# ALiBi attention: the distance bias of two heads at once by 64x64 quarter tiles, with smaller identity multiples

## The chip, the cores and the metric

The kernel runs on one core of one Trainium2 chip. The metric is device time in microseconds, from one launch of the program; less is better. TensorE (PE), VectorE (DVE), ScalarE (ACT) and GpSimd (POOL) run side by side and are ordered by semaphores; SyncE (SP) only issues transfers. PEld is TensorE's weight load, PE its matmul.

## The reference

Six layers follow each other on x (16 sequences, 256 tokens, 128 features): a local-attention feed-forward block, an ALiBi attention, the same feed-forward block again, a mixture of experts, a linear attention, the experts again. Only the ALiBi attention matters here. Per sequence it has 16 heads of width 8:

```python
scores = jnp.einsum('bhid,bhjd->bhij', q, k) / scale
scores = scores + _alibi_bias(N_HEADS, seq_len, M_SLOPE, x.dtype)[None]   # -|i - j| * 0.5**h
attn = jax.nn.softmax(scores, axis=-1)
out = jnp.einsum('bhij,bhjd->bhid', attn, v)
```

## The kernel before

The program is written out by hand for each engine, with semaphores between them: `ffn(0)`, `attn()`, `ffn(1)`, `moe(0)`, `lin()`, `moe(1)`. There is no planner; each engine issues its instructions in the order of its own Python loop.

The set-up comes first. `shape_constants` computes tables on the host; the part up to `slope_eye` is loaded into the tile `stage` by one transfer of ScalarE's queue (L812), followed on the same queue by small loads (`lo_q`, `lo_k`, `block`, q and k scales). VectorE waits for all of them (L848) and converts the parts to bf16: masks (L851), `relub` (L852), `sel` (L853), `slopeb` (L854), and goes on with the tables and weights until the first `ffn` starts at about 60 us.

In `attn()` all three engines run a loop over k (a sequence, in -2 to 19) and p (8 steps, two heads each). In a step TensorE computes two things (`scores`, L1559). The *plain* scores of sequence k, heads 2p and 2p+1, go to PSUM banks 0 and 1: q is the stationary operand, so rows are queries; VectorE takes their row maximum (`s_max`, L1068), which frees the banks for step p+1. The *turned* scores, of heads that lie 11 steps back (u = 8k + p - 11), go to banks 4 and 5 with keys on the rows; ScalarE takes their exponential (`exps`, L692), which frees them. Every score product has a contraction of 32 rows (8 of q high, q low, position and maximum rows), and the row group of a head is given by its number, so that plain and turned products of four heads lie in four different groups of 32 rows of the array.

The linear part of the bias, -m|i-j| for the off-diagonal blocks, comes in with the position rows of these products. In the two diagonal blocks of 128x128 that form is wrong by 2m max(i-j, 0) or its mirror. This is mended by the distance products: the stationary operand is `slopeb[:, h, :]`, a 128x128 multiple -2m of the identity for head h, the moving one a 128x128 table `relub` of max(p-f, 0) or max(f-p, 0). There are four of them for the plain scores (two heads, two diagonal blocks, L1584) and four for the turned (L1591). The last of the four raises the semaphore on which `s_max` or `exps` waits.

After `scores`, the step's other work follows on TensorE (L1645 to L1665): `attend` (L1603) at odd p; `m_T` (L1616) and `proj` (L1641) at p = 0, `v_proj` (L1555) at 1, `mean` (L1531) and a half of `qk` (L1544 to L1547) at 2, the other half and `var` (L1535) at 4, `o_rows` (L1627) at 6, `o_cols` (L1636) at 7. VectorE adds to its maximum `m_add` (L1080) and `x_out` (L1092) at p = 0, `v_out` (L1061) at 1, `center` (L1047) at 2, `low` (L1056) at 3 and 5, `normed` (L1051) at 5, `o_norm` (L1086, L1087) at 6, `m_split` (L1074, L1075) at 7. ScalarE copies q and k (`high`, L687) at 3 and 5, before the exponentials of the step; the other copies (L697, L702) and `square`, `rstd` (L678, L682, L683) stand between them.

Of the kernel before, what the change touches and what calls it, by code (L numbers as in the profile page):

```python
# [20 lines left out]
BF16 = mybir.dt.bfloat16  # L21
# [4 lines left out]
SEQS, T, D = 16, 256, 128  # L26
LANES = 2
TILES = T // 128
P = 128
# [12 lines left out]
AH, ADH = 16, 8  # L42
# [22 lines left out]

def shape_constants():

    t = np.arange(T, dtype=np.float32)
    half = np.arange(0, DH, 2, dtype=np.float32)
# [12 lines left out]
    p, f = np.arange(P)[:, None], np.arange(P)[None, :]  # L82
# [30 lines left out]
    slope_eye = np.concatenate([-2.0 * m * eye for m in slopes], 1)  # L113
# [4 lines left out]
    parts = dict(rot=rot, masks=np.concatenate([st0, st1, s0, s1], 1), relu=np.concatenate([relu_pf, relu_fp], 1),  # L118
# [9 lines left out]
def build(nc, io, at):  # L128
    ctx = ExitStack()
    with ctx:  # L130
        def sb(name, shape, dt=F32, on=ctx):
            return on.enter_context(nc.sbuf_tensor(name, shape, dt))
# [40 lines left out]
        relub = sb("relu_bf", [P, 2, P], BF16)  # L173
        slopeb = sb("slope_eye_bf", [P, AH, P], BF16)
# [659 lines left out]
        def _(dve):  # L834
            steps = [0]

            def link(ins):

                steps[0] += 1
                ins.then_inc(chain, 1)  # L840
                dve.wait_ge(chain, steps[0])
# [10 lines left out]
            link(dve.tensor_copy(relub[:, :, :].rearrange("p a b -> p (a b)"), part("relu")))  # L852
# [438 lines left out]
        def _(pe):  # L1291
# [235 lines left out]
            def attn():  # L1527
# [30 lines left out]

                def scores(k, p, u):  # L1559
# [20 lines left out]
                    if plain:  # L1580
                        for b in range(2):
                            for t in range(TILES):
                                a = t * T + t * P
                                last = pe.matmul(PS[:, b, a:a + P], slopeb[:, 2 * p + b, :], relub[:, 1 - t, :],  # L1584
                                                 start=False, stop=True, skip_group_check=True)
                        last.then_inc(a_s, 1)
                    if turned:
                        for b in range(2):
                            for t in range(TILES):
                                a = t * T + t * P  # L1590
                                last = pe.matmul(PS[:, 4 + b, a:a + P], slopeb[:, 2 * r + b, :], relub[:, t, :],  # L1591
                                                 start=False, stop=True, skip_group_check=True)
                        last.then_inc(a_st, 1)
# [280 lines left out]
```

## Time and profile before

| | |
|---|---|
| Median of 3 runs | 2494.72 us (2492.01 to 2496.49) |
| Profiled execution | 2494.18 us, its span 2492.4 us |
| PE busy | 2238.0 us (90%), 21606 products |
| PEld busy | 1670.2 us (67%) |
| DVE busy | 1709.9 us (69%) |
| ACT busy | 1465.2 us (59%) |
| POOL busy | 1095.6 us (44%) |
| Distance products, plain (L1584) | 53.0 us, 512 records, mean 229 ns |
| Distance products, turned (L1591) | 50.1 us, 512 records, mean 221 ns |
| TensorE's granted clock | 0.952 of full on average |

A product's record covers its own passage through the array, so the records of neighbouring products overlap and their sum is more than the time that they take. In the order of time, neighbouring instructions of one line are merged into one row with their number (x4); its start is that of the first and its length runs to the end of the last. Of a row the bracket at the end says how long the engine was idle before it, and what released it. A share of 1.00 in the clock's column is 2.4 GHz, 0.50 is 1.2 GHz. The attention stage lies between about 905 and 1280 us.

### The profile page before, as it was taken

The numbers are of one execution on the slowest core, as the hardware profiler recorded it, in microseconds if no ns is written. First come the engines' busy times: TensorE is split into PE (matmuls) and PEld (weight loads), VectorE is DVE, ScalarE is ACT, GpSimd is POOL, SyncE is SP. The second block draws the span as 40 slices with busy tenths as digits, with TensorE's granted clock in tenths as the row PEclk, the third lists the DMA queues.
The fourth block names the chain that finished last, engine by engine and source line by source line (L and its number), as shares of the span: only waits on it lengthen the run. The fifth ranks groups of instructions, "written<-read, shape, count | busy, mean of one in ns | idle before, by whom it ended". The sixth has DMA issues, their size and how long they took to land. (4 is left out here: it accounts for less than half of the span.)

```text
span 2492.4 us, 52712 instructions
## 1 busy us (share of the span) xinstructions
PE 2238.0 (90%) x21606; PEld 1670.2 (67%) x21606; DVE 1709.9 (69%) x2815; ACT 1465.2 (59%) x2389; POOL 1095.6 (44%) x800
## 2 busy tenths in 40 slices
PE   1799999999999969999969999999999997597968
PEld 1577777777777646666646777777777775495758
DVE  3677777778888636777737777777788784563556
ACT  0476767666676515555546677766676664363635
POOL 4655555656555210000025565656555560550245
PEclk8799999999999969999989999999999998698979
DMA  7000000069999970000000000000000002221022
GB/s 152 1 1 1 2 1 1 1 76 119 131 147 147 147 85 1 2 2 2 2 1 1 2 1 1 1 2 2 1 2 1 1 1 68 55 70 38 33 74 81
DMA packets 211362, 90.88 MB, mean 36 GB/s; under 512 B 79700, under 2 KB 206721, under 8 KB 210996
## 3 DMA queue, kind: packets, MB, share of 16 engines
q1 hardware_dynamic: 202596, 72.27, 21.8%
q0 software_dynamic: 6080, 11.76, 1.5%
q10 hardware_dynamic: 2448, 3.48, 0.7%
q8 instruction: 173, 2.83, 0.5%
q14 instruction: 65, 0.53, 0.1%
HBM read 24.51 MB, written 63.41 MB: 35 GB/s over the span
## 5 line engine op out<-in xcount | busy, mean ns | idle before, releaser
L477 POOL TENSOR_TENSOR work<-work,rot_tables 128x512 f32<-128x512 f32 x256 | 446.5, 1764 | 440.7 <-ACT work L581 440.7
L485 POOL TENSOR_TENSOR work<-work 128x1024 f32<-128x1024 f32 x128 | 305.2, 2384 | 13.0 <-DVE work L911 3.1
L911 DVE TENSOR_TENSOR work<-work,rot_tables 128x1024 f32<-128x1024 f32 x128 | 162.2, 1268 | 112.2 <-ACT work L581 112.2
L1068 DVE TENSOR_REDUCE small<-psum 128x4 f32<-128x1024 f32 x128 | 156.5, 1223 | 95.5 <-PE psum L1584 95.4
L1310 PE MATMUL psum<-qkv_w_hi,h_hi 128*128 128x512 f32 x384 | 182.7, 476 | 18.9 <-POOL h_lo L504 16.4
L1464 PE MATMUL psum<-centered,ffn_w 128*128 128x256 f32 x768 | 190.3, 399 | 6.1 <-DVE centered L972 2.9
L928 DVE TENSOR_TENSOR work<-work,small 128x1024 f32<-128x1024 f32 x128 | 159.5, 1248 | 51.2 <-ACT small L595 47.0
L692 ACT ACTIVATE work<-psum 128x1024 f32<-128x1024 f32 x128 | 131.2, 1025 | 102.2 <-PE psum L1591 102.2
L1402 PE MATMUL psum<-work 64*128 64x128 f32 (+1 forms) x2048 | 180.8, 307 | 0.0
L492 POOL TENSOR_TENSOR y_all<-centered,squared 64x256 f32<-64x256 f32 x64 | 48.7, 761 | 295.0 <-ACT squared L641 292.4
L1464 PEld LDWEIGHTS psum<-centered,ffn_w 128*128 128x128 f32 x768 | 145.8, 196 | 36.2 <-DVE centered L972 17.7
L1435 PE MATMUL psum<-work,v 128*32 128x192 f32 (+1 forms) x4096 | 162.9, 299 | 0.0
L609 ACT ACTIVATE work<-psum 128x768 f32<-128x768 f32 (+1 forms) x192 | 154.6, 872 | 3.6 <-PE psum L1402 3.5
L917 DVE TENSOR_REDUCE small<-qk_squares 128x16 f32<-128x1024 f32 x128 | 154.7, 1208 | 0.4 <-ACT qk_squares L586 0.4
L1312 PE MATMUL psum<-qkv_w_hi,h_lo 128*128 128x512 f32 x384 | 153.2, 399 | 0.0
L1311 PE MATMUL psum<-qkv_w_lo,h_hi 128*128 128x512 f32 x384 | 153.1, 399 | 0.0
L601 ACT ACTIVATE work<-psum 128x1024 f32<-128x1024 f32 x64 | 65.7, 1026 | 144.8 <-PE psum L1329 144.8
L546 POOL DMA_INDIRECT h_area<-rows,position x64 | 62.2, 972 | 199.7 <-DVE position L1150 173.4
L1402 PEld LDWEIGHTS psum<-work 64*128 64x128 f32 x2048 | 144.1, 189 | 0.0
L581 ACT ACTIVATE work<-psum 128x1024 f32<-128x1024 f32 x128 | 130.3, 1018 | 22.3 <-PE psum L1312 21.5
L750 ACT ACTIVATE qk_squares<-psum,work 128x128 f32<-128x128 f32 x312 | 89.0, 368 | 89.7 <-PE psum L1725 89.7
L528 POOL CAST h_hi<-centered 128x256 fp32r<-128x256 f32 x16 | 6.3, 396 | 302.9 <-DVE centered L1051 302.9
(285 smaller groups left out, 5718.6 us busy)
## 6 DMA issues: line engine op xcount, KB each, us to landing
h_area<-mean_weights SPq DMA_DIRECT2D x24, 2048.0 KB
tile_x<-h_area SPq DMA_DIRECT2D x39, 128.5 KB, 2.1
stage<-in_consts ACTq DMA_DIRECT2D x1, 3009.0 KB, 12.6
tile_x<-h_area SPq DMA_DIRECT2D x39, 64.5 KB, 1.8
work<-in_x SPq DMA_DIRECT2D x4, 512.0 KB, 27.4
expert_w<-in_ew SPq DMA_DIRECT2D x1, 2048.0 KB, 8.6
expert_w<-in_ew SPq DMA_DIRECT2D x8, 256.0 KB, 6.9
work<-y_tokens SPq DMA_DIRECT2D x4, 512.0 KB, 6.1
```

Source lines behind the costliest of these rows:

```text
L477: last = pool.tensor_tensor(b[:, :, :, o_], a[:, :, :, i_], tab[:, l, 1, t, :, o_].unsqueeze(2).to_broadcast([P, 2, HEADS, 32]), ALU.mult)
L485: pool.tensor_tensor(rC[:, t, :], rC[:, t, :], rB[:, t, :], ALU.add).then_inc(f_sum, 1)
L609: act.activation(PT[:, hs, a:a + w].rearrange("p (h b) j -> p b h j", b=2), PS[:, bs, 0:m * w].rearrange("p b (h j) -> p b h j", h=m), ACT ...
L911: dve.tensor_tensor(g(rC[:, t, :]), g(rA[:, t, :]), tab[:, l, 0, t, :, :].unsqueeze(2).to_broadcast([P, 2, HEADS, DH]), ALU.mult)\
L917: dve.tensor_reduce(sm[0][:, 16 * t:16 * t + 16], sq[:, t, :].rearrange("p (g d) -> p g d", d=DH), AX, ALU.add).then_inc(f_ss, 1)
L928: dve.tensor_tensor(c_, c_, sm[0][:, 96 + 16 * t:112 + 16 * t].unsqueeze(2).to_broadcast([P, 16, DH]), ALU.mult).then_inc(f_nrm, 1)
L1068: dve.tensor_reduce(dst, PS[:, 0:2, :].rearrange("p b (t j) -> p b t j", t=TILES), AX, ALU.max, negate=True).then_inc(a_smax, 1)
L1310: pe.matmul(out, hi, w_hi, start=True, stop=False)
L1312: return pe.matmul(out, lo, w_hi, start=False, stop=True)
L1402: last = pe.matmul(PS[:, bs[h % 2], o:o + w], kT[rows_(h), h // 2, j * P:(j + 1) * P], qT[rows_(h), h // 2, i0:i0 + w], start=False, stop= ...
L1435: last = pe.matmul(PS[32 * q:32 * q + 32, (4, 2)[a], z * T + lo:z * T + hi], V[i % 2][:, j, d:d + 32], PT[:, 4 * a + q, src:src + hi - lo] ...
L1464: last = pe.matmul(PS[:, b, o:o + T], fw[:, l, o2 + c * P:o2 + (c + 1) * P], ycen[:, :], start=True, stop=True)
```

## The change

Both tables are laid out anew and the distance products are issued on quarters of the array.

`slope_eye` holds 64x64 multiples of the identity instead of 128x128 ones: in rows 0 to 63 those of the even heads, in rows 64 to 127 those of the odd, 8 pairs x 64 columns (512 columns instead of 2048). `relu` holds max(p-f, 0), max(f-p, 0), max(p-f, 0) side by side, its upper 64 rows once for both row halves and then its lower 64 rows for both (768 columns instead of 256).

`distances` issues four products where there were four: for each half of the output rows and each of the two heads one with a contraction of 64 rows, 64 output rows and 256 columns, which are both diagonal blocks of the head (blocks 0 and 3 of the bank's four blocks of 128). The head gives the row half of the array and the bank, the half of the output gives the column half of the array. The order is half 0 of both heads, then half 1 of both. The semaphore is raised by the last, as before.

```diff
--- before.py
+++ after.py
@@ -61,6 +61,11 @@
 EPS = 1e-5
 MASKED = -1e30
 LN_SET = "natural_log_exp_and_others"
+
+
+def halves_of(a):
+
+    return np.concatenate([np.tile(a[0:64], (2, 1)), np.tile(a[64:P], (2, 1))], 1)
 
 
 def shape_constants():
@@ -110,12 +115,12 @@
             k_cols[2, c, r + ROW_MHI] = k_cols[2, c, r + ROW_MLO] = 1.0
         lo_q[r + 8:r + 16] = -1.0
         lo_k[r + 16:r + 24] = -1.0
-    slope_eye = np.concatenate([-2.0 * m * eye for m in slopes], 1)
+    slope_eye = np.concatenate([np.concatenate([-2.0 * m * eye[0:64, 0:64] for m in slopes[r::2]], 1) for r in range(2)], 0)
     block = (p // LDH == f // LDH).astype(np.float32)
     order = np.tile(np.arange(NE, 0, -1), (P, 4))
     before = (p < f).astype(np.float32)
     row_no = np.tile(np.repeat(np.arange(ROWS), NE), (P, 1))
-    parts = dict(rot=rot, masks=np.concatenate([st0, st1, s0, s1], 1), relu=np.concatenate([relu_pf, relu_fp], 1),
+    parts = dict(rot=rot, masks=np.concatenate([st0, st1, s0, s1], 1), relu=halves_of(np.concatenate([relu_pf, relu_fp, relu_pf], 1)),
                  q_cols=q_cols.reshape(P, -1), k_cols=k_cols.reshape(P, -1), q_vals=q_vals, k_vals=k_vals, lo_row=lo_row,
                  sel=sel.reshape(P, -1), slope_eye=slope_eye, eye=eye, lo_q=lo_q, lo_k=lo_k, block=block, order=order, before=before, row_no=row_no)
     at, n = {}, 0
@@ -170,8 +175,8 @@
         ms0, ms1 = masks[:, JW:JW + P], masks[:, JW + P:2 * JW]
         sel = sb("m_rows_bf", [P, HEADS, P], BF16)
         tab = sb("rot_tables", [P, DEPTH, 2, TILES, 2, DH])
-        relub = sb("relu_bf", [P, 2, P], BF16)
-        slopeb = sb("slope_eye_bf", [P, AH, P], BF16)
+        relub = sb("relu_bf", [P, 2, 3, P], BF16)
+        slopeb = sb("slope_eye_bf", [P, AH // 2, 64], BF16)
         lo_q, lo_k = sb("lo_q", [P, 1]), sb("lo_k", [P, 1])
         block = sb("block", [P, P])
         raw_qk = work[1][:, 4 * 4 * P:6 * 4 * P]
@@ -849,7 +854,7 @@
             link(dve.tensor_copy(eyeb[:, :], eye[:, :]))
             link(dve.memset(mneg[:, :, :], 0.0))
             link(dve.tensor_copy(masks[:, :], part("masks")))
-            link(dve.tensor_copy(relub[:, :, :].rearrange("p a b -> p (a b)"), part("relu")))
+            link(dve.tensor_copy(relub[:, :, :, :].rearrange("p a k b -> p (a k b)"), part("relu")))
             link(dve.tensor_copy(sel[:, :, :].rearrange("p h j -> p (h j)"), part("sel")))
             link(dve.tensor_copy(slopeb[:, :, :].rearrange("p h j -> p (h j)"), part("slope_eye")))
 
@@ -1556,6 +1561,15 @@
                                          start=True, stop=True)
                     last.then_inc(a_v, 1)
 
+                def distances(b0, pair, first):
+                    for half in range(2):
+                        for r in range(2):
+                            k_, o_ = slice(64 * r, 64 * r + 64), slice(64 * half, 64 * half + 64)
+                            blocks = PS[o_, b0 + r, :].rearrange("p (a c) -> p a c", c=P)[:, 0::3, :]
+                            last = pe.matmul(blocks, slopeb[k_, pair, :], relub[k_, half, first:first + 2, :],
+                                             start=False, stop=True, skip_group_check=True)
+                    return last
+
                 def scores(k, p, u):
                     plain, turned = 0 <= k < SEQS, 0 <= u < 8 * SEQS
                     m, r = u // 8, u % 8
@@ -1578,19 +1592,9 @@
                                 pe.matmul(PS[:, 4 + b, t * T:(t + 1) * T], ks[m % 3][row(r, b), r // 2, t * P:(t + 1) * P],
                                           qs[m % 3][row(r, b), r // 2, :], start=t == 0, stop=False, skip_group_check=True)
                     if plain:
-                        for b in range(2):
-                            for t in range(TILES):
-                                a = t * T + t * P
-                                last = pe.matmul(PS[:, b, a:a + P], slopeb[:, 2 * p + b, :], relub[:, 1 - t, :],
-                                                 start=False, stop=True, skip_group_check=True)
-                        last.then_inc(a_s, 1)
+                        distances(0, p, 1).then_inc(a_s, 1)
                     if turned:
-                        for b in range(2):
-                            for t in range(TILES):
-                                a = t * T + t * P
-                                last = pe.matmul(PS[:, 4 + b, a:a + P], slopeb[:, 2 * r + b, :], relub[:, t, :],
-                                                 start=False, stop=True, skip_group_check=True)
-                        last.then_inc(a_st, 1)
+                        distances(4, r, 0).then_inc(a_st, 1)
 
                 def attend(w):
                     k, c = w // 4, w % 4
```

## Rows read from the trace of the kernel before

**Rows 1.** Stretches of the attention stage: us, busy us (x instructions) of PE, PEld, DVE, ACT, POOL; PEclk, DMA, GB/s
```profile
966.00:1250.00 284.00, 265.98 (x3354) 191.21 (x3350) 208.81 (x251) 166.75 (x210) 13.43 (x24) 1.00 0.01 2
905.00:966.00 61.00, 48.62 (x414) 37.16 (x414) 35.14 (x40) 16.71 (x21) 3.35 (x6) 0.72 0.13 16
```

**Rows 2.** Order of time, PE: start us, us, engine, line; the proj product, eleven sequences apart
```profile
978.65 0.43 PE L1641 MATMUL psum<-work,attn_w_vo 128*128 128x256 f32 x1
...
1213.66 0.43 PE L1641 MATMUL psum<-work,attn_w_vo 128*128 128x256 f32 x1
```

**Rows 3.** Order of time, PE and PEld: scores and distance products of step p = 2
```profile
1046.29 0.39 PE L1574 MATMUL psum<-k_slots,q_slots 32*128 32x256 f32 x2
...
1046.52 0.28 PE L1578 MATMUL psum<-q_slots,k_slots 32*128 32x256 f32 x2
...
1046.72 0.23 PEld L1584 LDWEIGHTS psum<-relu_bf,slope_eye_bf 128*128 128x128 bf16 x4
1046.73 0.40 PE L1584 MATMUL psum<-relu_bf,slope_eye_bf 128*128 128x128 bf16 x4
...
1046.96 0.39 PE L1591 MATMUL psum<-relu_bf,slope_eye_bf 128*128 128x128 bf16 x4
...
1047.13 0.30 PEld L1531 LDWEIGHTS psum<-x_all,mean_weights 128*128 128x128 f32 x2
```

**Rows 4.** Order of time, PE: changes of tile form and waits in other steps
```profile
1044.33 0.39 PE L1591 MATMUL psum<-relu_bf,slope_eye_bf 128*128 128x128 bf16 x4
1044.64 1.07 PE L1603 MATMUL psum<-work 128*32 128x256 f32 x16
...
1053.07 0.36 PE L1544 MATMUL psum<-h_hi,attn_w_hi 128*128 128x256 f32 x1
...
1062.39 0.44 PE L1636 MATMUL psum<-eye,work 128*128 128x128 f32 x2
```

**Rows 5.** Order of time, DVE, of one sequence
```profile
1042.26 1.23 DVE L1068 TENSOR_REDUCE small<-psum 128x4 f32<-128x1024 f32 x1 [0.52 <-PE psum L1584]
1043.40 1.21 DVE L1080 TENSOR_TENSOR q_slots<-q_slots,psum 128x1024 fp32r<-128x1024 f32 x1
...
1044.93 1.22 DVE L1068 TENSOR_REDUCE small<-psum 128x4 f32<-128x1024 f32 x1
...
1051.69 1.27 DVE L1056 SCALAR_TENSOR_TENSOR q_slots<-q_slots,lo_q,psum 128x1024 fp32r<-128x1024 f32 x1
...
1056.45 1.23 DVE L1068 TENSOR_REDUCE small<-psum 128x4 f32<-128x1024 f32 x1 [2.35 <-PE psum L1584]
...
1059.12 1.22 DVE L1068 TENSOR_REDUCE small<-psum 128x4 f32<-128x1024 f32 x1
...
1061.27 1.23 DVE L1068 TENSOR_REDUCE small<-psum 128x4 f32<-128x1024 f32 x1 [0.21 <-PE psum L1584]
```

**Rows 6.** Order of time, ACT, step p = 3
```profile
1049.78 1.02 ACT L687 ACTIVATE q_slots<-psum 128x1024 fp32r<-128x1024 f32 x1 [1.37 <-PE psum L1547]
1050.78 1.02 ACT L692 ACTIVATE work<-psum 128x1024 f32<-128x1024 f32 x1
```

**Rows 7.** Order of time, PE and ACT, a turned step after the last plain one
```profile
1253.51 0.40 PE L1591 MATMUL psum<-relu_bf,slope_eye_bf 128*128 128x128 bf16 x4
...
1253.94 1.02 ACT L692 ACTIVATE work<-psum 128x1024 f32<-128x1024 f32 x1 [0.92 <-PE psum L1591]
```

**Rows 8.** Set-up: a stretch, then VectorE's first conversions in order of time
```profile
0.00:10.00 10.00, 0.00 (x0) 0.00 (x0) 0.00 (x0) 0.00 (x0) 9.15 (x14) 1.00 0.82 303
...
34.62 0.23 DVE L849 CAST eye_bf<-eye 128x128 bf16<-128x128 f32 x1 [34.62 <-DMA qk_squares<-in_k_scale]
...
35.66 0.29 DVE L852 CAST relu_bf<-stage 128x256 bf16<-128x256 f32 x1
...
36.72 1.23 DVE L854 CAST slope_eye_bf<-stage 128x2048 bf16<-128x2048 f32 x1
```

**Rows 9.** A stretch before the body of the stage (columns as in rows 1)
```profile
955.00:960.00 5.00, 4.24 (x68) 2.53 (x60) 3.72 (x5) 2.52 (x4) 0.00 (x0) 0.91 0.00 0
```

## Prediction

> **What bounds the kernel now.** I read the busy share of TensorE first, then its share and clock by stretches, then the order of instructions inside one sequence of the attention stage. TensorE is the busiest engine of the whole program (90% of the span, in the table above). The change touches only two places: the set-up of the constants (the first 60 us) and the ALiBi stage, which runs from 905 us to 1280 us. In the body of that stage (966 to 1250 us) TensorE is busy 266 of 284 us at full clock, VectorE 209 and ScalarE 167 [rows 1]; in its head the clock is half of the time the low one (0.72 on average). So at first sight TensorE sets the pace, but 94% is an average over eight unlike steps, and what a shorter product is worth depends on what each step waits for.
>
> The body is strictly periodic: eleven sequences between two launches of the same projection take 1213.66 - 978.65 = 235.0 us, 21.37 us each [rows 2]. One sequence has eight steps p. A step issues eight score products in 32-row tiles, four distance products of the plain scores (L1584), four of the turned ones (L1591), and then the step's other work: an attend product at odd p, and m_T and proj, mean and qk, qk and var, o_rows at p = 0, 2, 4, 6.
>
> **The parts of one step.** S is the start of the step's scores, 1046.29 in [rows 3]. There the second set of score products starts at S+0.23 and its 256 columns at 2.4 GHz (clock 1.00) are streamed 0.107 us later, at S+0.34. The first weight load of the distance products comes at 1046.72 = S+0.43: 0.09 to 0.10 us in which nothing streams, because the array passes from 32-row tiles to the full array. The four plain products (4 in 0.40 us, 0.22 of it one product's own record, so 0.06 apart) end at S+0.84, the turned ones at S+1.06. The next load in the same full form follows at once (1047.13 = S+0.84). Where the next work has another tile form it follows later: L1591 ends at 1044.33+0.39 = 1044.72, its last product started 0.22 before that, at 1044.50, streamed 0.05, and L1603 starts at 1044.64, again 0.09 late [rows 4]; the turned group ended there at S+1.06, so L1603 starts at about S+0.99. So a change of form costs 0.10 us, seen in both directions.
>
> **What the change makes of it.** Each group of four 128-column products over the full array becomes four of 256 columns, each on a 64x64 quarter. The trace has no 64x64 product, so I bound it. From below: if all four quarters run together, a group is 256 columns = 0.107 us, against 4 x 0.055 = 0.22 us now; it can't be less. The nearest rows are for running together: four 32-row tiles (two rows of two products, 0.01 us apart, [rows 3]) and four 32-column tiles (16 products of L1603 in 1.07 us [rows 4], where 16 one after the other at the same 256 columns of two-pass f32 would take 3.4 us). Rows are split in the one and columns in the other; both at once is not shown. From above: two at a time 0.215 us, one at a time 0.43 us. I take 0.107 us, since both halves of the claim are shown. The first load in a new form is exposed: for 128 columns of f32 it makes the first score record 0.10 us longer than the second (0.38 against 0.28 [rows 3]). For 64 columns I take 0.05, with 0 and 0.10 as ends.
>
> Then a step becomes: load at S+0.43, plain group streamed by S+0.43+0.05+0.107+0.01 (three starts after each other) = S+0.60, its end 0.17 later (a 128-column record of 0.22 less its 0.053 of streaming), S+0.77 instead of S+0.84: **0.07 us earlier for VectorE's maximum**. The turned group ends 0.11 later, at S+0.88 instead of 1.06: **0.18 earlier for ScalarE's exponentials**. The array is free for another form at S+0.71+0.10 = S+0.81. At odd p, where another form follows anyway, this is 0.18 before the present 0.99. At even p the change adds a change of form that wasn't there: the f32 load now begins at S+0.84 and its product streams 0.107 later, S+0.95; afterwards S+0.81+0.107 = S+0.92, only **0.03 earlier**.
>
> The Trainium skill, TensorEngine Tiling (Array Packing), "Key Properties", says that a change of tiling mode drains the engine; this speaks against the change at the even steps, and the trace agrees with its 0.10 us. The Trainium skill, TensorE: Matmul & The Clock Gate, "Measured speedup vs the span model", has row and column tiles composed, at about 4 ns a tile; no run here shows it, and by it the group would be the 0.107 us plus 0.01. The same page, "Weight-path perf modes", gives the fast load only to 128 columns, and in "LDWEIGHTS" a load of its columns over 1.2 GHz, an estimate of 0.053 us for 64; the sum would be the same by it.
>
> **Which of this lies on the path, step by step.** A step starts when the later of three is there: TensorE free, the maximum of the step before (0.14 us after its end), the exponentials of the step before.
> - p = 0 to p = 2: the maximum of p = 0 (1042.26), m_add L1080 (1043.40), x_out L1092 and the maximum of p = 1 (1044.93 + 1.22 = 1046.15) are one unbroken chain on VectorE [rows 5], and 0.14 later p = 2 starts, at 1046.29. TensorE would have been ready at the same moment; it gains 0.27 here and gets 0.07. Gain 0.07.
> - p = 2 to 3: the qk block on TensorE, an even step. 0.03.
> - p = 3 to 4: ScalarE copies q high (1049.78 + 1.02) and only then does the exponentials (1050.78) [rows 6]; the earlier product is hidden by the copy. 0.
> - p = 4 to 5: the qk block (L1544 at 1053.07 [rows 4]) waits for `low` (1051.69 + 1.27 [rows 5]), which stands behind the maximum of p = 3. 0.07.
> - p = 5 to 7: from the maximum of p = 5 (1056.45) over `low` and `normed` to the maximum of p = 6 (1059.12) VectorE is unbroken [rows 5]. 0.07.
> - p = 7 to 0: TensorE: attend, then o_cols (1062.39 [rows 4]), then scores; odd step, 0.18. VectorE's maximum (1061.27 + 1.23 + 0.14 = 1062.64) is 0.11 behind at present and 0.07 earlier too, so it doesn't stop it.
> Sum 0.42 us of 21.37. The stretch in which plain and turned run together, 942 to 1249 us, has 14 such periods: **5.9 us**. TensorE alone saves 4 x 0.18 + 4 x 0.03 = 0.84 a period; half of it is lost to VectorE and ScalarE.
>
> Head: 11 steps of plain scores alone; in some 8 the maximum sets the pace, 0.07 each, 0.5 us (at the low clock everything doubles and the gain is no smaller). Tail: 11 turned steps, L1591 at 1253.51 and exponentials at 1253.94 [rows 7]. The four products now take 0.43 to that point; then it is 0.05 + 0.107 + 0.01 + 0.17 + 0.03 = 0.37. 11 x 0.06 = **0.7 us**.
>
> Set-up: VectorE converts the constants in an unbroken chain from 34.62 us on. slope_eye shrinks from 2048 to 512 columns, relu grows from 256 to 768. The two conversions (0.29 for 256 and 1.23 for 2048 columns, hence 0.52 us per 1000) fall from 1.52 to 0.42 + 0.56 us: **0.5 us** [rows 8]. The stage load loses 1024 columns, 0.52 MB; at the 303 GB/s of the first 10 us that is 1.7 us of transfer. The chain starts on the last of the small loads behind it, which may follow by all of it or by nothing; I take 0.8.
>
> Sum 5.9 + 0.5 + 0.7 + 0.5 + 0.8 = 8.4 us. The profiled execution took 2494.18 us (span 2492.4 and 1.8 around it), so 2485.8; the median of the runs is 0.5 higher, which gives **2486.3 us**. Ends of its own: load exposed for 0 and the whole transfer gained, 0.04 us more on four links of a period and each loop, 8.4 + 2.2 + 1 + 0.9 = 12.5, 2482; load 0.10 (0.05 more on each: -3.5) and nothing from the transfer, 4.1 us, 2490.6. Own range 2482 to 2491.
>
> **Rivals.**
> - *Two quarters at a time.* A group takes 0.215. The plain group ends at S+0.88 (0.04 later than now), exponentials start 0.02 later, odd steps are 0.03 and even ones 0.17 later. By the same links: 0.04 + 0.17 + 0.02 + 0.04 + 0.04 + 0.03 = 0.34 a period, 14 x 0.34 + 1 less 1.3 for the set-up = 4.5 us slower, 2499. Against it stand the two rows of four tiles together; for it only that the mix is not shown. The point of balance lies at about 0.165 us a group.
> - *One at a time*: 0.43 a group. Then TensorE bounds every step: loops through the exponentials grow by 0.45, even steps by 0.60. Some 3.3 us a period, 14 x 3.3 + 6 - 1 = 51 us slower, 2546. This is the case clearly on the other side; it decides as soon as quarters that share rows or columns exclude each other, which no row suggests.
> - *The clock falls inside the body.* TensorE would be busy some 88% instead of 94%. The clock was 0.91 in a stretch of 5 us with 4.24 us busy [rows 9], and it stayed full through the whole body, with 94%. If it fell in one qk block of each sequence, 16 products of 256 columns would take 0.107 us more each, 1.7 us: 14 x 1.7 = 24, less 8 gives 16 us slower, 2510. Against it: the columns that each quarter streams grow, only the time shrinks.
> - *VectorE absorbs more than I give it*: only the set-up and the ends remain, and 0.1 to 0.2 a period: 4 us faster, 2491.
> - That the quarters aren't used as such (the products fall back to the full array) comes out as one at a time.
>
> **Chances.** Forecast 0.60, VectorE absorbs 0.12, two at a time 0.15, the clock 0.07, one at a time 0.03, better than 2481 0.03. What a measurement of this kernel can tell from no change is about 0.2%, 5 us: 2489.7 and 2499.7 are the borders. Faster: nine tenths of the forecast, a third of the absorbed case, the 0.03: 0.62. Slower: the clock, one at a time and a third of two at a time, 0.15. Same 0.23. For 8 in 10 the range takes in two at a time: 2481 to 2500.
>
> **What would show it.** In the changed profile: the four quarter records of a group starting within 0.02 us of each other and the second group 0.11 after the first (right) or 0.2 and more (rival); the first load of the group 0.10 after the scores; the maximum at S+0.80, the exponentials at S+0.92; a period of 20.95 us; p = 3 to 4 unchanged; clock 1.00 from 966 to the end of the body; the conversion of slope_eye in 0.4 us and the chain starting near 33.8. A period over 21.3 or a low clock in the body would prove me wrong.

## The result, and the profile after

The changed kernel took 2486.93 us (median), the kernel before 2495.12 us in the same comparison: 8.2 us less by the medians; the ratio is 0.9971 [0.9961, 0.9981], which is 7.2 us. One of the ten executions of each kernel ran far longer than its others (7251.18 and 2851.13 us): they are in these medians, but not in the ratio. The profiled execution took 2481.03 us, with a span of 2478.9 us. The forecast was 2486.3 us. The sum hit the total; several of its terms were off, in both directions, and those are what the experiments were for. The kernels before and after have two profiles each, the other forms one, and a form whose time isn't given below was executed once and is read by its trace alone.

The stretch 966 to 1250 us of [rows 1] can't be laid beside the same stretch of the changed kernel, because the stage starts 4 us earlier and is shorter, so that this stretch now holds most of its tail. What does compare is the proj product (order of time, TensorE), against [rows 2]:

```profile
969.39 0.43 PE L1645 MATMUL psum<-work,attn_w_vo 128*128 128x256 f32 x1
...
1197.64 0.43 PE L1645 MATMUL psum<-work,attn_w_vo 128*128 128x256 f32 x1
```

Eleven sequences take 1197.64 - 969.39 = 228.25 us: **a period of 20.75 us**. Before the change it was 21.37, and 20.95 had been forecast. The step p = 2, all engines in order of time, against [rows 3] and the second row of VectorE's chain in [rows 5]:

```profile
1013.11 1.22 DVE L1073 TENSOR_REDUCE small<-psum 128x4 f32<-128x1024 f32 x1
...
1014.38 0.39 PE L1588 MATMUL psum<-k_slots,q_slots 32*128 32x256 f32 x2 [0.16 <-DVE small L1073]
...
1014.61 0.28 PE L1592 MATMUL psum<-q_slots,k_slots 32*128 32x256 f32 x2
1014.82 0.14 PEld L1569 LDWEIGHTS psum<-relu_bf,slope_eye_bf 64*64 64x64 bf16 x8
1014.82 0.41 PE L1569 MATMUL psum<-relu_bf,slope_eye_bf 64*64 64x256 bf16 x8
1015.16 0.30 PEld L1536 LDWEIGHTS psum<-x_all,mean_weights 128*128 128x128 f32 x2 [0.20 <-issue]
...
1015.17 1.23 DVE L1073 TENSOR_REDUCE small<-psum 128x4 f32<-128x1024 f32 x1 [0.49 <-PE psum L1569]
1015.28 1.03 ACT L697 ACTIVATE work<-psum 128x1024 f32<-128x1024 f32 x1 [1.63 <-PE psum L1569]
```

With S = 1014.38, the maximum starts at S+0.79 (before: 1042.26 - 1041.39 = 0.87), the exponentials at S+0.90 (before: 1047.39 - 1046.29 = 1.10, ScalarE), the next full-array load at S+0.78 (before S+0.84). The eight products of both groups span 0.41 us, where the two groups of four took from 1046.73 to 1047.35.

The tail (turned steps alone) and the set-up answer [rows 7, 8], in order of time:

```profile
1237.28 0.30 PE L1569 MATMUL psum<-relu_bf,slope_eye_bf 64*64 64x256 bf16 x4
...
1237.64 1.02 ACT L697 ACTIVATE work<-psum 128x1024 f32<-128x1024 f32 x1 [0.84 <-PE psum L1569]
```

```profile
31.80 0.23 DVE L854 CAST eye_bf<-eye 128x128 bf16<-128x128 f32 x1 [31.80 <-DMA qk_squares<-in_k_scale]
...
32.85 0.56 DVE L857 CAST relu_bf<-stage 128x768 bf16<-128x768 f32 x1
...
34.17 0.43 DVE L859 CAST slope_eye_bf<-stage 128x512 bf16<-128x512 f32 x1
```

The two conversions now take 0.99 us instead of 1.52, as forecast. In the tail it is 0.36 us from products to exponentials instead of 0.43, with 0.37 forecast, and a step takes 1.86 us (1236.85 to 1238.71) instead of 1.94 (1253.08 to 1255.02). This is at full clock; later in the same tail a step takes 2.95 us (1245.61 to 1248.56) in a stretch at the low clock.

**The stage in three parts** (head, body, tail). I cut it at the first turned score product, the last plain one, and the first product of the next stage. Before, then after (us, busy us (x instructions) of PE, PEld, DVE, ACT, POOL; PEclk, DMA, GB/s):

```profile
905.30:941.30 36.00, 27.64 (x158) 22.19 (x158) 19.28 (x22) 3.13 (x5) 2.24 (x4) 0.59 0.21 25
941.30:1249.00 307.70, 285.96 (x3588) 205.50 (x3590) 223.70 (x266) 180.20 (x224) 14.55 (x26) 0.99 0.01 2
1249.00:1280.00 31.00, 23.67 (x253) 13.96 (x249) 6.24 (x12) 16.88 (x20) 0.00 (x0) 0.94 0.01 1
```

```profile
901.30:935.00 33.70, 25.39 (x162) 18.98 (x162) 19.28 (x22) 3.13 (x5) 2.24 (x4) 0.65 0.22 28
935.00:1233.10 298.10, 266.23 (x3591) 169.53 (x3590) 222.71 (x266) 178.78 (x224) 14.54 (x26) 0.99 0.01 2
1233.10:1265.10 32.00, 24.99 (x252) 13.04 (x249) 6.33 (x12) 16.88 (x20) 0.00 (x0) 0.84 0.01 1
```

Two profiles of before (head, body, tail 36.0, 307.7, 31.0 and 35.8, 306.0, 29.8) have means 35.9, 306.9, 30.4. Four of the quarter form (33.7, 298.1, 32.0; 33.9, 297.5, 35.1; 34.0, 297.5, 35.1; 34.0, 298.3, 32.0: this one, again, pad and eight, below) have 33.9, 297.9, 33.6. So **the body gives 9.0 us, the head 2.0, the tail takes 3.2 back**, and with 0.5 from the conversions that is 8.3 us. TensorE's clock in the tail is 0.84 and 0.72 in the changed forms, 0.94 and 1.00 before. In the first profile of the changed kernel the low clock lies here:

```profile
1224.00:1230.80 6.80, 5.58 (x64) 2.25 (x56) 3.22 (x3) 3.32 (x4) 0.00 (x0) 0.50 0.01 2
1241.10:1251.30 10.20, 9.07 (x70) 4.79 (x68) 0.00 (x0) 4.69 (x5) 0.00 (x0) 0.50 0.00 0
```

The first of the two is still in the body, and the steps in it take 2.23, 2.59 and 3.16 us instead of 2.07 each, 1.8 us in all. The three other profiles of the quarter form have low clock in the same place.

### The profile page after: what moved, and what is told of

The parts are those of the page before. It is cut to its first block and busy times, and to the rows that moved or that the text cites. A ratio compares the mean times of both kernels' runs of the same rounds, so it can differ in the third digit from the quotient of the medians.

```text
span 2478.9 us, 52712 instructions
## 1 busy us (share of the span) xinstructions
PE 2222.0 (90%) x21606; PEld 1634.3 (66%) x21606; DVE 1710.0 (69%) x2815; ACT 1464.7 (59%) x2389; POOL 1094.9 (44%) x800
## 3 DMA queue, kind: packets, MB, share of 16 engines
q10 hardware_dynamic: 2448, 2.95, 0.6%
## 5 line engine op out<-in xcount | busy, mean ns | idle before, releaser
L697 ACT ACTIVATE work<-psum 128x1024 f32<-128x1024 f32 x128 | 131.0, 1024 | 90.6 <-PE psum L1569 90.3
L591 ACT ACTIVATE qk_squares<-work 128x1024 f32<-128x1024 f32 x128 | 135.4, 1058 | 2.0
```

## Experiments

The period below is always the one between two proj products eleven sequences apart.

**again**: the changed kernel once more.

> The changed kernel once more, to set the body of the attention stage against the rest. The body must show the 20.75 us period again. Theory A (14 periods of 0.62 us and the shorter conversions, 9.2 us, arrive at the end): ratio 0.9963. Theory B (some of it is given back where the clock is low for part of the time, in the ends of this stage and in the expert stages after 2080 us, because their low stretches fall differently from run to run): ratio 0.9975 to 0.999, and the trace has more low-clock time after 2080 us than the 105 us of before. First conversion somewhere in 31.8 to 34.6 us, with no relation to the size of the transfer.

2494.32 us against 2501.72 us, ratio 0.9968 [0.9955, 0.9982], period 20.75 (967.08 to 1195.32). The gain is there again. The interval holds the ratios of both theories (0.9963, 0.9975), so it doesn't decide between them. From the end of the stage to the end of the program the profiles of the changed kernel take 1213.8 and 1222.4 us (again), those of the kernel before 1212.4 and 1219.1 (before2): what lies behind the stage varies by as much as the gain.

**before2**: the kernel before once more, for its stage.

> The kernel before once more, word for word, for a second profile of it. Theory A (start of the conversions and length of the expert stages vary from run to run, whatever the kernel): first conversion between 31.7 and 33.2 us as in all other runs rather than at 34.6, and from 2080 us on a time or low clock unlike the first profile's, period 21.37 all the same. Theory B (both belong to the kernel before): 34.6 us again, and the shortest expert stages.

Period 21.36 (975.13 to 1210.08), time 2496.34; the first conversion of the set-up starts at 32.81 us, where it was 34.62 in the first profile of the same program. So the start of VectorE's chain moves by 1.8 us, and the part behind the stage (above) by 6.7 us, from one execution to another of the same kernel.

**pad**: 1024 unused columns in the stage load, so that it is as large as before.

```diff
-    parts = dict(rot=rot, masks=..., relu=halves_of(...),
+    parts = dict(rot=rot, masks=..., relu=halves_of(...), pad=np.zeros((P, 1024)),
```

> The changed kernel with 1024 columns of zeros added to the set-up transfer, so that it is as long as before; nothing else differs. Theory A (the shorter transfer lets VectorE's first conversion start at 31.8 us instead of 34.6): the start goes back to 34.3 to 34.9 and the first product of the feed-forward block comes at 59.6 instead of 56.8 us (before 60.2); the whole run loses 2.8 us of the gain, about 5.5 us faster than before, ratio 0.9978. Theory B (the start varies from run to run whatever the length): it stays near 31.8, the ratio near 0.9967.

The first conversion starts at 32.88 us; in the changed kernel it was 31.80 and 31.71 (again), in others with the small load 32.98 (plain_only) and 32.18 (eight). That is neither theory's number. Beside the 1.8 us by which before itself moves, one pair of profiles can't tell what the 0.52 MB costs. Over all fourteen profiles of this page, the five with the load of before (before, before2, before_halfmax, pad, and rows_only with its wider table) start between 32.25 and 34.62 us, 33.14 on average, and the nine with the small load between 31.71 and 33.00, 32.24 on average. The 0.9 us between the averages is near the 0.8 that I took, but the two ranges overlap, so the effect is likely and not shown. The time was 2489.98 against 2492.61, ratio 0.9992 [0.9978, 1.0007], and that I can't explain: its period is 20.75, its stage 366.6 us, within 0.1 of that of again, and its profiled execution (2489.76 us) took what again's did (2489.89). What differs between the two comparisons, on the same chip, is the kernel before, 2492.61 in one and 2501.72 in the other. It stays open whether the padding costs something outside the stage or whether the kernel before was at its best there. The part behind the stage doesn't single pad out: 1218.7 us, between the two profiles of the changed kernel.

**plain_only** and **turned_only**: only one of the two groups uses quarters; the other uses the old full-array products, with tables built in the set-up.

```diff
-                        distances(4, r, 0).then_inc(a_st, 1)
+                        distances_full(4, r, True).then_inc(a_st, 1)    # plain_only
...
-                        distances(0, p, 1).then_inc(a_s, 1)
+                        distances_full(0, p, False).then_inc(a_s, 1)    # turned_only
```

> Only the plain distance products by quarters, the turned ones as before, over the full array (their tables are built by 18 more small VectorE instructions in the set-up, some 4 us, so only the period of the stage is compared). Theory A (a change of tile form costs 0.10 us, and now stands between the two groups too): the maximum starts at S+0.80 as in the changed kernel, but the exponentials at S+1.13, later than before (1.10); the period is 21.34 us, hardly better than the 21.37 before. Theory B (each group brings its half of the gain, 0.31 us): 21.06.

> Only the turned distance products by quarters, the plain ones as before (same longer set-up). Theory A (form change between the groups): maximum at S+0.87 as before, exponentials at S+1.12, period 21.4 us, no better than the 21.37 before. Theory B (each group brings half): 21.06.

Periods 21.23 (977.86 to 1211.43) and 21.56 (976.52 to 1213.63): of the 0.62 the one half alone gives 0.14, and the other makes the period 0.19 longer than before (21.34 and 21.4 had been expected). plain_only, order of time, an odd step with S = 1042.49:

```profile
1042.92 0.30 PE L1576 MATMUL psum<-relu_bf,slope_eye_bf 64*64 64x256 bf16 x4
1043.15 0.23 PEld L1584 LDWEIGHTS psum<-tile_y,tile_x 128*128 128x128 bf16 x4
1043.16 0.40 PE L1584 MATMUL psum<-tile_y,tile_x 128*128 128x128 bf16 x4
...
1043.59 1.02 ACT L699 ACTIVATE work<-psum 128x1024 f32<-128x1024 f32 x1 [1.25 <-PE psum L1584]
```

turned_only, S = 1042.01:

```profile
1042.46 0.40 PE L1584 MATMUL psum<-tile_y,tile_x 128*128 128x128 bf16 x4
1042.78 0.30 PE L1576 MATMUL psum<-relu_bf,slope_eye_bf 64*64 64x256 bf16 x4
...
1043.14 1.02 ACT L699 ACTIVATE work<-psum 128x1024 f32<-128x1024 f32 x1 [1.27 <-PE psum L1576]
```

Both have a change of form between the groups. In turned_only four full products take 4 x 0.055 = 0.22 from 1042.46; with the change of 0.10 that is 1042.78, where the quarter group starts. The exponentials start at S+1.10 and S+1.13, no better than before (1.10). Together, the two groups pay one change of form into the quarters and one out of them; with one group on the full array there is one more change between them, and the gain is eaten. This rules out 21.06, which an even split of the gain would give. One group by itself occupies 0.30 us, both 0.41: the second follows 0.11 us behind.

**rows_only**: halves of 64 rows by all 128 columns, with zeros beside the identity, so that only two products can run together.

```diff
-                            blocks = PS[o_, b0 + r, :]....[:, 0::3, :]
-                            last = pe.matmul(blocks, slopeb[k_, pair, :], ...
+                            blocks = PS[:, b0 + r, :]....[:, 0::3, :]
+                            last = pe.matmul(blocks, slopeb[k_, pair, 64 - 64 * half:192 - 64 * half], ...
```

> Each distance product keeps its 64 rows of contraction and its 256 columns, but its stationary operand is 128 wide, the other half zeros: tiles of 64x128, of which only two fit side by side. This is the rival of two at a time. Theory A (products share the array only if their tiles don't overlap; the form with both halves is what pays): a group takes 0.22 instead of 0.13 us, maximum at S+0.89, exponentials at S+1.11, period 21.6 us, slower than before. Theory B (what pays is the smaller contraction or the fewer, longer products): period near the 20.75 of the changed kernel.

Order of time, S = 1036.70:

```profile
1037.13 0.61 PE L1570 MATMUL psum<-relu_bf,slope_eye_bf 64*128 64x256 bf16 x8
...
1037.68 0.85 PE L1608 MATMUL psum<-work 128*32 128x256 f32 x12
```

Eight products occupy 0.61 instead of 0.41 us, the next form comes at S+0.98, and the period is 21.46 (971.52 to 1207.61): 0.09 longer than before. So with two at a time the period would have been longer, as the rival had it, though by less than its 0.34, and the gain needs all four quarters to run together.

**eight**: the same quarters, eight products of 128 columns a group instead of four of 256.

```diff
-                    for half in range(2):
-                        for r in range(2):
-                            blocks = PS[o_, b0 + r, :]....[:, 0::3, :]
+                    for t in range(TILES):
+                        for half in range(2):
+                            for r in range(2):
+                                last = pe.matmul(PS[o_, b0 + r, 3 * P * t:3 * P * t + P], ...
```

> The changed kernel with the two diagonal blocks of a head as two products of 128 columns: eight products of 64x64 per group instead of four of 256 columns, block by block, so that neighbours lie on different quarters. Theory A (the quarters make the gain; the longer product only saves instructions): the group still holds the array for two times 128 columns, 0.12 to 0.14 us, period 20.75 to 20.85 us. Theory B (each product has a price of its own that a longer one spreads): the group takes 0.2 us and more, period 21.2 to 21.5.

Period 20.76 (970.06 to 1198.42), with 16 products in 0.42 us:

```profile
1012.85 0.42 PE L1569 MATMUL psum<-relu_bf,slope_eye_bf 64*64 64x128 bf16 x16
```

Putting both diagonal blocks into one product gives nothing by itself; the quarters give it all. (Its time, 2496.71, was taken once, so I go by the stage alone.)

**none**: all distance products left out; the stage then computes attention without the bias.

```diff
-                        distances(0, p, 1).then_inc(a_s, 1)
+                        last_p.then_inc(a_s, 1)
-                        distances(4, r, 0).then_inc(a_st, 1)
+                        last_t.then_inc(a_st, 1)
```

> The changed kernel without any distance products: the last score product raises the semaphore (the diagonal blocks keep the wrong bias). It tells what is left to gain and what bounds it. Theory A (VectorE's chains set the starts at p = 0 to 2, 3 to 5 and 5 to 7): maximum and exponentials at S+0.54, other work at S+0.44; links 4.47 + 2.98 + 5.56 + 4.47 + 1.88 = 19.36 us a period. Theory B (TensorE is the bound, each of eight steps gains the 0.34 us that the products hold it): 18.0.

Between 974.96 and 1189.77 the period is 19.53. At full clock it is 19.40 (19.36 had been expected), and elsewhere in the body the clock has fallen (proj at two places two sequences apart, in order of time, then the stretch 940 to 1200):

```profile
1013.75 0.65 PE L1645 MATMUL psum<-work,attn_w_vo 128*128 128x256 f32 x2
...
1052.55 0.65 PE L1645 MATMUL psum<-work,attn_w_vo 128*128 128x256 f32 x2
```

```profile
940.00:1200.00 260.00, 218.70 (x2440) 147.41 (x2441) 202.19 (x244) 160.92 (x207) 14.54 (x26) 0.96 0.01 1
```

Leaving the products out altogether saves 1.97 us a period, so the change takes 0.62 of what could be had. With TensorE busy 218.7 of 260 us, 84%, the clock was 0.96, where the changed kernel's body has 89% (266.2 of 298.1) at 0.99 and before's 93% at 0.99. So a clock that falls inside the body, the rival of the prediction, is what this form shows.

**before_halfmax** and **after_halfmax**: VectorE's maximum reads only the two diagonal blocks, half of its elements, in either kernel; the maximum is then not that of the whole row.

```diff
-    dve.tensor_reduce(dst, PS[:, 0:2, :].rearrange("p b (t j) -> p b t j", t=TILES), AX, ALU.max,
+    dve.tensor_reduce(dst, PS[:, 0:2, :].rearrange("p b (t j) -> p b t j", j=P)[:, :, 0::3, :], AX, ALU.max,
```

> The kernel before with the maximum taken over the two diagonal blocks alone, 512 of 1024 columns (so the stabiliser isn't the row maximum): VectorE's 1.22 us becomes about 0.66. Theory A: the loops of before are held by TensorE and ScalarE at p = 0 to 3, so only the waits for low and the step 6 to 7 gain: 4.90 + 3.39 + 2.24 + 3.40 + 2.24 + 2.24 + 2.36 = 20.8 us a period. Theory B (VectorE bounds most steps of before): below 20.

> The changed kernel with the same halved maximum. Theory A (VectorE takes half of what the quarters bring): with VectorE out of the way the steps are held by the exponentials (S+0.90+1.02+0.11 = 2.04) and TensorE: 2.04 + 2.42 + 3.32 + 2.16 + 3.37 + 2.04 + 2.04 + 2.15 = 19.5 us, a gain of 1.2 to 1.3 us a period over the kernel before with a halved maximum, twice the 0.62 of the real pair. Theory B (VectorE takes nothing): the gain stays near 0.6.

Order of time, TensorE, first in before_halfmax, then in after_halfmax:

```profile
966.24 0.43 PE L1641 MATMUL psum<-work,attn_w_vo 128*128 128x256 f32 x1
...
1195.48 0.43 PE L1641 MATMUL psum<-work,attn_w_vo 128*128 128x256 f32 x1
```

```profile
967.83 0.43 PE L1645 MATMUL psum<-work,attn_w_vo 128*128 128x256 f32 x1
...
1183.65 0.43 PE L1645 MATMUL psum<-work,attn_w_vo 128*128 128x256 f32 x1
```

Periods 20.84 and 19.62. With VectorE's maximum halved the same change gives 1.22 us a period instead of 0.62. That shows where the other half of what the quarters could bring goes in the real pair: into VectorE's chain, as the prediction said. The 1.22 us is more than the 0.84 that the prediction gave to TensorE alone. Step by step, five of the eight links gain 0.20 us here (2.27 to 2.07 four times over, and 2.36 to 2.15), also at the even steps p = 0 and 6, for which it had 0.03: there the next step waits for the exponentials, and these start 0.20 earlier. A step that is shared by two nearly equal engines gives back only what both can follow.

**filled**: in the head and the tail, where TensorE idles, three idle products of 512 columns (some 0.65 us at full clock) into banks that nothing uses at that time.

```diff
+                    if turned != plain and (p in (0, 3, 5, 6, 7) if plain else u % 2 == 1):
+                        if turned:
+                            pe.wait_ge(a_smax, 8 * SEQS)
+                        for n in range(3):
+                            pe.matmul(PS[:, (0 if turned else 4) + n % 2, :], eyeb[:, :], masks[:, 0:4 * P],
+                                      start=True, stop=True)
```

> The changed kernel with three idle products of 512 bf16 columns (0.65 us) in those steps of the head and the tail of the attention stage in which TensorE waits over a microsecond; their results are never read. Theory A (in head and tail low clock costs time, and comes from TensorE's waits: 24 us of the head and 34 to 44 us from the tail on are low): the granted clock there rises towards 1.00, the tail to the next stage takes 66 to 69 us instead of 69 to 73, the head 31 instead of 33.7; ratio to before 0.994 to 0.996, where the changed kernel has 0.997. Theory B (the clock is no matter of these waits, or the filling takes more than it gives): ratio 0.997 or more.

The three parts of the stage:

```profile
901.90:934.80 32.90, 27.55 (x180) 18.69 (x180) 19.26 (x22) 3.13 (x5) 2.24 (x4) 0.79 0.37 29
934.80:1234.50 299.70, 268.15 (x3589) 171.36 (x3590) 222.70 (x265) 178.77 (x224) 14.57 (x26) 0.98 0.01 2
1234.50:1264.60 30.10, 25.69 (x270) 13.00 (x266) 6.34 (x12) 16.87 (x20) 0.00 (x0) 0.96 0.00 1
```

The tail's clock is back at 0.96 and the tail at 30.1 us; the head has a clock of 0.79 and takes 32.9 us. 2487.63 us against 2502.07, ratio 0.995 [0.9933, 0.9967]. With the same work and 18 idle products more, the tail is shorter at the higher clock, so it is the clock that took the 3.2 us back. Why the clock fell in the changed kernel isn't shown. The obvious reason is that the quarters leave TensorE less to do in the tail, and two forms speak against that as the whole of it. turned_only has the same turned quarters in its tail, and there all eleven turned steps ran at full clock:

```profile
1249.00:1273.80 24.80, 19.55 (x240) 10.35 (x240) 5.29 (x10) 15.13 (x18) 0.00 (x0) 1.00 0.01 2
1249.23:1279.80 30.57, 23.21 (x252) 12.51 (x249) 6.35 (x12) 16.86 (x20) 0.00 (x0) 0.90 0.01 1
```

rows_only has steps of 1.94 us there at full clock, as long as those of before, and yet a tail of 34.6 us at 0.78. And the first low stretch of the changed kernel (1224.0) comes before the tail; in filled it is absent, though the idle products of the tail stand behind that place. Whether the whole kernel gains is less clear, because the intervals of filled and again overlap and the stage is only 1.1 us shorter than in the first profile of the changed kernel, 3.8 than in again's.

**filled_bound**: filled, and for all pairs of heads but the first the plain distance products are left out, and the last plain score product releases the maximum. The distances are never positive, so the maximum over scores without them is at least the true one, and the softmax is the same with any such bound. The turned scores keep theirs. The first pair, whose slopes are the steepest, keeps both groups.

```diff
-                        distances(0, p, 1).then_inc(a_s, 1)
+                        (distances(0, p, 1) if p < 1 else last_p).then_inc(a_s, 1)
```

> The filled kernel, and in steps p = 1 to 7 the plain distance products are left out and the last plain score product releases the maximum. The bias without its mending is never lower, and for these heads at most 0.5*254 = 127 x 0.5 = 63.5 too high, so the stabiliser stays an upper bound of the row's maximum, and the softmax is the same. Theory A (the links as read): maximum at S+0.54 in these steps, exponentials at S+0.78, links 4.73 + 3.22 + 5.56 + 4.47 + 2.05 = 20.03 us a period instead of 20.75, 10 us more over the stage; ratio 0.990 to 0.992. Theory B (TensorE's lower activity lets the clock fall in the body and takes it back): period well above 20.1 or a clock under 1.00 in the body, ratio 0.996.

Order of time, p = 2, with S = 1035.66:

```profile
1035.66 0.38 PE L1588 MATMUL psum<-k_slots,q_slots 32*128 32x256 f32 x2 [0.27 <-DVE small L1073]
...
1036.20 1.23 DVE L1073 TENSOR_REDUCE small<-psum 128x4 f32<-128x1024 f32 x1 [0.27 <-PE psum L1588]
...
1036.45 1.03 ACT L697 ACTIVATE work<-psum 128x1024 f32<-128x1024 f32 x1 [1.63 <-PE psum L1569]
```

The maximum starts at S+0.54 instead of S+0.79, the period is 20.02 (972.11 to 1192.33), the body 289.4 us, and the time 2476.7 against 2502.07: **0.9907 [0.989, 0.9925], better than both kernels**. This pays 0.73 us a period, more than the quarters themselves. It takes a group of products from TensorE and the wait for it from VectorE at once, so it doesn't tell by itself which of the two pays.

## Why the prediction was right, and where its terms were off

**What bounds the kernel, and the links.** Scores to scores, in one sequence of either kernel (before 1041.39, 1043.65, 1046.29, 1049.68, 1051.94, 1055.58, 1057.85, 1060.40, 1062.75; after 1009.65, 1011.73, 1014.38, 1017.69, 1019.88, 1023.52, 1025.59, 1028.25, 1030.40), the gain of each link is:

| link | forecast | measured |
|---|---|---|
| p = 0 to 2 | 0.07 | 4.90 - 4.73 = 0.17 |
| p = 2 to 3 | 0.03 | 3.39 - 3.31 = 0.08 |
| p = 3 to 5 | 0 + 0.07 | 5.90 - 5.83 = 0.07 |
| p = 5 to 7 | 0.07 | 4.82 - 4.73 = 0.09 |
| p = 7 to 0 | 0.18 | 2.35 - 2.15 = 0.20 |
| sum | 0.42 | 0.61 |

- *All four quarters together, 0.107 us a group*: right. One group occupies 0.30 us (plain_only), of which one product's record is 0.27 to 0.29, so four start within 0.03; the second follows 0.11 later. The Trainium skill, TensorE: Matmul & The Clock Gate, "Measured speedup vs the span model", puts row and column tiles together at some 4 ns a tile; the trace agrees with it: the first four quarter products of step p = 2 start within 0.01 us of each other.
- *The first load of 64 columns, 0.05 us*: too much. The next form's load at S+0.78 less the first product's S+0.44, two groups of 0.107 and the change of 0.10 leaves 0.03 for the exposed load and the spread of the starts, where I had 0.06. This gives the even step 0.06 instead of 0.03, measured 0.08. The same page's "LDWEIGHTS" has columns over 1.2 GHz, an estimate of 0.053 us; of that, the trace shows 0.03 exposed at most.
- *A change of form 0.10 us in each direction*: right; 1042.46 to 1042.78 in turned_only is the 0.22 of streaming and 0.10.
- *Maximum at S+0.80, exponentials at S+0.92*: 0.79 and 0.90.
- *The release of a step, 0.14 us after VectorE's maximum*: this step failed. In the changed kernel the maximum ends at 1013.11 + 1.22 = 1014.33 and the scores start at 1014.38, 0.05 later. The 0.14 seen before in the unbroken chain of [rows 5] was not VectorE's: I wrote that TensorE would have been ready at the same moment, and should have followed it: v_proj held TensorE until the scores began, and the step started when that was done. Another step of the same trace has it right: the maximum of 1016.39 + 1.22 = 1017.61 us, TensorE idle for 0.36, and scores at 1017.66. From p = 0 to 2 the link is 0.07 from the maximum and 0.09 from this, 0.17 (4.73 = 0.80 + 2.66 + 1.22 + 0.05). This is the largest error, 0.10 of 0.19.
- *p = 3 to 5*: the sum is right, the split isn't. From p = 3 to 4 came 0.07, not 0. I had the copy of q high hold the exponentials [rows 6]; but before the change they started at S+1.10 (1050.78 - 1049.68), as in every other step, and it was the turned group that held them. Now the copy does: they start at S+1.03, 0.10 before the copy's recorded end, and the scores of p = 4 0.14 after their own end (1018.72 + 1.02 = 1019.74 to 1019.88). ScalarE, order of time, S = 1017.69:

```profile
1017.80 1.02 ACT L692 ACTIVATE q_slots<-psum 128x1024 fp32r<-128x1024 f32 x1 [1.49 <-PE psum L1552]
1018.72 1.02 ACT L697 ACTIVATE work<-psum 128x1024 f32<-128x1024 f32 x1
```

  From p = 4 to 5 came 0 instead of 0.07, since p = 5 hangs on `low`, which follows the maximum of p = 3 and is 0.07 earlier against p = 3, whenever p = 4 starts.
- *Half of TensorE's saving goes to VectorE*: right in kind, and shown by the pair with a halved maximum. In size it is 0.62 of 1.22, where the forecast had 0.42 of 0.84. (The 0.27 that it gave TensorE from p = 0 to 2 is 0.21 by its own 0.18 and 0.03; nothing hangs on it.)
- *Body*: 14 x 0.61 = 8.5 us by this, 9.0 measured between the cuts, 5.9 forecast.
- *Head*: 2.0 instead of 0.5 us. That the maximum sets the pace there is right. A step at the low clock, before and after, order of time, TensorE:

```profile
930.38 0.79 PE L1574 MATMUL psum<-k_slots,q_slots 32*128 32x256 f32 x4 [1.41 <-DVE small L1068]
...
933.03 0.80 PE L1574 MATMUL psum<-k_slots,q_slots 32*128 32x256 f32 x4 [0.47 <-DVE small L1068]
```

```profile
925.17 0.80 PE L1588 MATMUL psum<-k_slots,q_slots 32*128 32x256 f32 x4 [1.43 <-DVE small L1073]
...
927.66 0.80 PE L1588 MATMUL psum<-k_slots,q_slots 32*128 32x256 f32 x4 [0.37 <-DVE small L1073]
```

  It falls from 2.65 to 2.49 us, by 0.16; at full clock a step falls from 2.15 to 2.07, by 0.08. I had priced all of them at 0.07. Six such steps, four of them at the low clock, give 0.8 us. Most of the rest lies in two steps that ran at different clocks in the two profiles: the first (2.65 us at 0.50, then 2.07 at 0.95) and the last (5.64 at 0.50, then 4.82 at 0.61). In before2 these take 2.25 and 4.84, so what they give depends on where the low clock falls, and the forecast has no such term.
- *Tail*: +3.2 instead of -0.7 us. At full clock the forecast was right: 0.36 from products to exponentials for 0.37, and 0.08 a step for 0.06. The step that failed is the clock: I priced the tail at that of before (0.94) and put the clock rival into the body only. That the clock takes the 3.2 us is shown by filled; why it fell stays open, as said there.
- *Conversions* 0.5 us: right (1.52 to 0.99). *Transfer* 0.8 us: likely by the averages of fourteen profiles (0.9 us), but not shown.

So it was luck that the forecast fell within 0.7 us of the median: 3.1 and 1.5 us too little in body and head against 3.9 too much in the tail, with the 0.8 of the transfer open.

**The rivals.** Two at a time: excluded by 0.11 between groups; rows_only shows that it would have been slower, as said. One at a time, and products that don't use the quarters: excluded by the same row. The clock in the body: the prediction named a low clock there as a sign of being wrong, and it did come, for 6.8 us at the end of the body (1224.0 to 1230.8), at a cost of 1.8 us instead of the rival's 24. The first profile of before has 3.4 us of it in its body too (952.5 to 955.9), before2 has none. The eleven sequences that give the period are free of it. VectorE absorbs more: excluded by the period.

## What to carry to other kernels

Where two engines alternate in a loop of nearly equal length, cost a shorter product link by link, and for each gap ask which engine was the later one: a gap behind an unbroken chain on one engine isn't its release time if another engine was busy up to the same moment. Look at the granted clock of each stretch, and not only of the body, before and after: here the tail's fell in all four profiles of the quarter form and took back more than the tail had to give. Put products of one tile form next to each other: the gain of quarters was there only when both groups used them.

## What the runs showed of the hardware

- Four products on 64x64 quarters that differ in rows and columns stream together: a group every 0.11 us for 256 columns of bf16, against 0.22 us for the same work in full-array products, and 16 products of 128 columns in 0.42 us, no slower than eight of 256 in 0.41.
- From the end of a VectorE instruction to TensorE's next product 0.05 us (before 1017.61 to 1017.66; after 1014.33 to 1014.38); from the end of ScalarE's exponentials to it 0.14 us (before 1042.49 + 1.02 = 1043.51 to 1043.65; after 1019.74 to 1019.88).
- In the tail of the stage the length goes with TensorE's granted clock: 29.8 us at 1.00 and 31.0 at 0.94 before the change, 32.0 at 0.84 and 35.1 at 0.72 with the quarters, 30.1 at 0.96 with idle products added. The same step takes 1.86 us at full clock and 2.95 at the low one.
